# A ring of four load slots, other waits for the loads and a moved store wait in the ternary weight preparation of a Mamba-plus-BitLinear kernel

## The chip, the cores and the metric

One Trainium2 chip, eight cores. All cores run the same program on different data: core b gets sequence b of the input (2048 tokens of 1024 features) and its own copy of all weights. Nothing is exchanged between the cores. The time of a run is the device time of the slowest core in microseconds.

## The reference, cut to what matters

```python
def attn(x, Wd, bd, a_log, b_param, Wo, bo):          # per sequence
    delta = softplus(x @ Wd.T + bd)
    a_pos = softplus(a_log) + 1e-4                    # 1024 x 16 states
    # for each t: state = exp(-dt * a_pos) * state + dt * b_param * x_t
    #             y_t   = state.sum(-1)
    return y @ Wo.T + bo

def weight_quant(w):                                  # ternary weights
    scale = 1.0 / clip(mean(abs(w)), 1e-5)
    return clip(round(w * scale), -1, 1) / scale

def act_quant(x):                                     # 8 bit activations, scale by row
    scale = 127.0 / clip(max(abs(x), axis=-1), 1e-5)
    return clip(round(x * scale), -128, 127) / scale

def bitlinear(x, w):
    return act_quant(x) @ weight_quant(w).T

def ffn(x, w_gate, w_up, w_down):                     # 1024 -> 4096 -> 1024
    return bitlinear(silu(bitlinear(x, w_gate)) * bitlinear(x, w_up), w_down)

x = x + layernorm(attn(layernorm(x)))
x = x + layernorm(ffn(layernorm(x)))
```

The three weights of the second half (gate and up 4096 x 1024, down 1024 x 4096, float32, 16 MB each) are made ternary on the chip. That needs two passes over each weight: one for the mean of the absolute values, one to quantize.

## The kernel before, in words

**Order of work.** Each engine runs its own list of instructions in the order in which the program adds them (the class `Sched`, L29). An instruction waits on counters: `ST(engine)` is "the last counted instruction of that engine added so far", `sch.chain(engine)` the same on its own engine, and a DMA has a counter for its buffer slot. All loads and stores told of here are issued by SyncE (SP), whose list is in order too: a DMA that waits holds back every DMA behind it, and an engine that waits holds back all its later instructions.

**Stages.** (1) LayerNorm of x, the delta projection, and the scan of the first quarter of the tokens. (2) The weights of gate (`wg`) and then up (`wu`) are prepared by `prep_ternary_gen`. The program takes one step of this generator, then adds one block `emit_B_dc(1, dc)` of the scan of the second quarter (16 states: an exponential on ScalarE, a scan and a multiply-add on VectorE, and on GpSimd the save of the last state), then the next step. There are only 8 such blocks, so they stand between the first 9 steps of `wg`; all steps behind them stand alone. (3) `emit_C_q(0)`: output projection and LayerNorm of the first quarter, with the preparation of the down weight (`wdn`) between: after each of its four token tiles 6 steps are taken, and the steps left are taken at the end. (4) For each quarter of the tokens: gate and up projections, quantization, down projection, final LayerNorm; with the scans of the third and fourth quarter between.

**One weight in `prep_ternary_gen`.** Its memory is a buffer `wbuf` of 2 slots, each of 2 tiles of 128 x 1024 float32 (one load fills a slot: 1 MB), `tern` for ternary tiles, and `stage` for 256 transposed output columns.

- First pass (L472 to L491), 16 steps, q = 0 to 15: SyncE loads slot q % 2 (L478); ScalarE takes absolute values and their sum (L483); GpSimd adds the sum to `acc` (L488). For q of 2 and above the load waits for `ST("gpsimd")`, the last GpSimd instruction added: the add of step q-1, or where a scan block stands between, the last save added in it. The absolute values wait for the load, for `ST("gpsimd")` as well, and for ScalarE itself.
- Scale (L493 to L513): a chain of small instructions on TensorE, ScalarE and VectorE.
- Second pass (L533 to L590), per output row pair `rp`: the 2 slots' worth of tiles of `rp` are loaded again (L544), shifted and rounded by L552, made -1, 0 or 1 by L557 (both ScalarE), transposed by TensorE in pairs (L573), copied to `stage` by ScalarE (L529), and `stage` is stored to DRAM by SyncE (L586). Then ScalarE waits for that store to land (L589), as `stage` is written again by the next `rp`. Each load of this pass waits for `ST("scalar")`.
- `CC` is the number of 1024-wide tiles in a row of the weight. For gate and up `CC` is 1: 16 `rp` with one load of 2 tiles each, 8 copies to `stage`, and a store of 512 KB. For down `CC` is 4: 4 `rp` with 4 loads each (2 per half), 32 copies, and a store of 2 MB.

Of the kernel before, what the change touches and what calls it, by code (L numbers as in the profile page):

```python
# [7 lines left out]
F32 = mybir.dt.float32  # L8
# [117 lines left out]
def build_nc(stop_phase=99):  # L126
# [24 lines left out]
    with ExitStack() as es:  # L151
        S = lambda n, sh, dt: es.enter_context(nc.sbuf_tensor(n, sh, dt))
        sch = Sched(nc, es)
        ST = sch.token
# [46 lines left out]
        with nc.sbuf_tensor("aw1", [128, KC * NSTATE], F32) as aw1, \  # L201
# [3 lines left out]
                    waits=[t_nega_ld])  # L205
            sch.add("scalar", lambda h: h.activation(out=aw1[:], in_=aw1[:], func=AF.Exp, scale=-1.0),
                    waits=[sch.chain("scalar")])
            sch.add("scalar", lambda h: h.activation(out=aw1[:], in_=aw1[:], func=AF.Ln, bias=1.0),
                    waits=[sch.chain("scalar")])
            sch.add("scalar", lambda h: h.activation(out=aw2[:], in_=av, func=AF.Relu), inc=1)  # L210
            sch.add("vector", lambda h: h.tensor_tensor(aw1[:], aw1[:], aw2[:], ALU.add),
                    waits=[ST("scalar")])
            sch.add("vector", lambda h: h.tensor_scalar(av, aw1[:], 1e-4, -1.0, ALU.add, ALU.mult),
                    waits=[sch.chain("vector")])
# [136 lines left out]
        with nc.sbuf_tensor("lnscA", [128, D], F32) as lnscA, \  # L351
# [3 lines left out]
            with nc.psum_tensor("ptA", [128, KC, 1024], BF16) as ptA:  # L355
                for tc in range(NC):
# [5 lines left out]
                            waits=[t_st], inc=1)  # L362
                    t_ln = ST("scalar")
                    for ic in range(KC):
                        w = []
                        if ic == 0:
                            w.append(t_ln)
                            if tc >= 1:
# [4 lines left out]
                                waits=w, inc=(1 if ic == KC - 1 else 0))  # L373
# [5 lines left out]
                            waits=[t_pe], inc=1)  # L379
# [4 lines left out]
            with nc.psum_tensor("pdA0", [128, 512], F32) as pdA0, \  # L384
# [5 lines left out]
                for g in range(4):  # L390
                    for ec in range(KC):
# [5 lines left out]
                        par = it % 2  # L397
                        for kc in range(KC):
                            w = []
                            if kc == 0:  # L400
# [6 lines left out]
                                    waits=w, inc=(1 if kc == KC - 1 else 0))  # L407
# [4 lines left out]
                                waits=[t_mm])  # L412
                        sch.add("scalar", lambda h: h.activation(out=spA0[:], in_=spA0[:],
                                                                 func=AF.Exp, scale=-1.0),
                                waits=[sch.chain("scalar")])
                        sch.add("scalar", lambda h: h.activation(out=spA0[:], in_=spA0[:],
                                                                 func=AF.Ln, bias=1.0),
                                waits=[sch.chain("scalar")])
# [9 lines left out]
                                waits=[t_sp, sch.chain("vector")])  # L428
                        sch.add("scalar", None, waits=[ST("vector")])
                    t_mmw = ST("tensor")  # L430
                    for d in range(KC):
# [4 lines left out]
                            waits=([t_mmw] if d == 0 else []) + [sch.chain("vector")])  # L436
# [13 lines left out]
        def prep_ternary_gen(d_wsrc, d_wT, O, I, wsc_col, name, es_w):  # L450
            RC = O // 128
            CC = I // 1024
# [5 lines left out]
            else:  # L458
                wv4_slice = lambda q: _wv[:, q // 2, 2 * (q % 2):2 * (q % 2) + 2, :]
            wTv = d_wT.rearrange("(ic p) o -> p ic o", p=128)  # L460
            Sx = lambda n, sh, dt: es_w.enter_context(nc.sbuf_tensor(n, sh, dt))
            wbuf = Sx(f"{name}_buf", [128, 2, 2, 1024], F32)
            acc = Sx(f"{name}_acc", [128, 2], F32)
            tern = Sx(f"{name}_tern", [128, 2, I], BF16)
            stage = Sx(f"{name}_stage", [128, IC, 256], BF16)
# [1 line left out]
            sch.barrier()  # L467
            sch.add("gpsimd", lambda h: h.memset(acc[:, 0:1], 0.0),
                    waits=[sch.chain("gpsimd")])
            for q in range(RC * CC // 2):  # L470
                par = q % 2
                w_dma = []  # L472
                if q >= 2:
                    w_dma.append(ST("gpsimd"))
                else:
                    w_dma += [ST("gpsimd"), ST("scalar")]
                sch.dma("sync", f"wbuf{par}",
                        lambda h, q_=q, p=par: h.dma_start(  # L478
                            out=wbuf[:, p, :, :], in_=wv4_slice(q_)),
                        waits=w_dma)  # L480
                t_d = (f"dma_wbuf{par}", sch.counts[f"dma_wbuf{par}"])
                sch.add("scalar",
                        lambda h, p=par: h.activation(  # L483
                            out=tern[:].rearrange("p a b -> p (a b)")[:, 0:2048],
                            in_=wbuf[:, p, :, :].rearrange("p a b -> p (a b)"),
                            func=AF.Abs, accum_out=acc[:, 1:2]),
                        waits=[t_d, ST("gpsimd"), sch.chain("scalar")])
                sch.add("gpsimd", lambda h: h.tensor_tensor(acc[:, 0:1], acc[:, 0:1],  # L488
                                                            acc[:, 1:2], ALU.add),
                        waits=[ST("scalar"), sch.chain("gpsimd")])  # L490
                yield  # L491
            with nc.psum_tensor(f"{name}_p1", [1, 1], F32) as p1, \
# [4 lines left out]
                        waits=[ST("gpsimd")], inc=1)  # L497
                sch.add("scalar", lambda h: h.copy(out=sc2[:, 0:1], in_=p1[:]),  # L498
                        waits=[ST("tensor"), sch.chain("scalar")])
# [3 lines left out]
                        waits=[ST("scalar"), sch.chain("vector")])  # L503
                sch.add("vector", lambda h: h.reciprocal(sc2[:, 1:2], sc2[:, 0:1]),
                        waits=[sch.chain("vector")])
                sch.add("tensor", lambda h: h.matmul(p2[:], s_onesk[:], sc2[:],
                                                     start=True, stop=True),
                        waits=[ST("vector")], inc=1)
                sch.add("scalar", lambda h, wc=wsc_col: h.activation(
                    out=s_wsc[:, wc:wc + 2], in_=p2[:], func=AF.Copy),  # L510
                    waits=[ST("tensor"), sch.chain("scalar")])
# [5 lines left out]
            with nc.psum_tensor(f"{name}_pta", [128, 2, 1024], BF16) as pta, \  # L517
                 nc.psum_tensor(f"{name}_ptb", [128, 2, 1024], BF16) as ptb:
                pts4 = (pta, ptb)
                TPD = max(2 // CC, 1)  # L520
                bi = 0
                t_pe_hist = {}
                evac_args = {}
                evac_tok = {}

                def emit_evac(k):
                    half_, bb_ = evac_args[k]
                    sch.add("scalar",
                            (lambda p, b, pp: lambda h: h.activation(  # L529
                                out=stage_v[:, b * 2:(b + 1) * 2, p, :],  # L530
                                in_=pts4[pp][:, :, 0:128], func=AF.Copy))(half_, bb_, k % 2),
                            waits=[t_pe_hist[k], sch.chain("scalar")])
                    evac_tok[k] = ST("scalar")  # L533

                for rp in range(RC // 2):
                    for half in range(2):
                        r = rp * 2 + half
                        for c in range(CC):
                            gt = r * CC + c
                            if gt % 2 == 0:  # L540
                                q = gt // 2
                                par4 = q % 2
                                sch.dma("sync", f"wbuf{par4}",
                                        lambda h, q_=q, p=par4: h.dma_start(  # L544
                                            out=wbuf[:, p, :, :], in_=wv4_slice(q_)),
                                        waits=[ST("scalar")])
                            q = gt // 2
                            par4 = q % 2
                            tl = gt % 2
                            t_d = (f"dma_wbuf{par4}", sch.counts[f"dma_wbuf{par4}"])  # L550
                            sch.add("scalar",
                                    lambda h, p=par4, t_=tl: h.activation(  # L552
                                        out=wbuf[:, p, t_, :], in_=wbuf[:, p, t_, :],
                                        func=AF.Identity, scale=swcol, bias=s_magic_ap),
                                    waits=[t_d, t_magic, ST("tensor"), sch.chain("scalar")])
                            sch.add("scalar",
                                    lambda h, p=half, c_=c, pp=par4, t_=tl: h.activation(  # L557
                                        out=tern[:, p, c_ * 1024:(c_ + 1) * 1024],
                                        in_=wbuf[:, pp, t_, :], func=AF.Sign, bias=s_negm_ap),
                                    waits=[ST("tensor"), sch.chain("scalar")])  # L560
                            yield
                        ternv = tern[:].rearrange("p b (ic q) -> p b ic q", q=128)
                        t_q = ST("scalar")
                        for bb in range(IC // 2):
                            ppar = bi % 2
                            for j in range(2):
                                w = []
                                if j == 0:
                                    w.append(t_q)
                                    if bi >= 2:  # L570
                                        w.append(evac_tok[bi - 2])
                                sch.add("tensor",
                                        lambda h, p=half, i=bb * 2 + j, j_=j, pp=ppar: h.transpose(  # L573
                                            pts4[pp][:, j_, 0:128], ternv[:, p, i, :], s_ident[:]),
                                        waits=w, inc=1)
                            t_pe_hist[bi] = ST("tensor")
                            evac_args[bi] = (half, bb)
                            if bi >= 1 and (bi - 1) not in evac_tok:
                                emit_evac(bi - 1)
                            bi += 1  # L580
                            yield
                    if (bi - 1) not in evac_tok:
                        emit_evac(bi - 1)
                    t_ev = ST("scalar")
                    t_st2 = sch.dma("sync", "stage_st",
                                    lambda h, rp_=rp: h.dma_start(  # L586
                                        out=wTv[:, :, rp_ * 256:(rp_ + 1) * 256], in_=stage[:]),
                                    waits=[t_ev])
                    sch.add("scalar", None, waits=[t_st2])  # L589
                    yield  # L590
            sch.pe_fence()

        def make_prep_driver(queue):
# [171 lines left out]
        with nc.sbuf_tensor("s_h", [128, 4, DI], BF16) as s_h, \  # L765
# [14 lines left out]
            for g in range(4):  # L780
                with ExitStack() as es_gu:
# [5 lines left out]
                    for oc in range(8):  # L787
                        for half in range(2):
# [17 lines left out]
                            for c in range(4):  # L806
                                tc = g * 4 + c
                                for k4 in range(4):
                                    kc = half * 4 + k4
                                    w = []  # L810
# [314 lines left out]
```

How the kernel before makes its waits and increments, by code:

```python
        def emit_engine(handle, eng):  # L95
            for fn, waits, inc, inc_sem in self.ops[eng]:
                for (wname, wval) in waits:
                    if wval > 0:
                        handle.wait_ge(sems[wname], wval)
                if fn is not None:
                    instr = fn(handle)
                    if inc:
                        instr.then_inc(sems[inc_sem], inc)
```

## Time and profile before

| | |
|---|---|
| median of 3 runs | 4353.5 us (4347.38 to 4356.2) |
| the profiled execution | 4356.49 us |
| its slowest core, first to last instruction | 4354.9 us (core 6; others 4322.2 to 4348.9) |
| busy on that core | TensorE 1305.4 us, VectorE 1498.0 us, ScalarE 1449.5 us, GpSimd 260.0 us |
| DMA | 245.36 MB, mean 56 GB/s |
| preparation of `wg` and the scan blocks beside it | about 639 to 1294 us |
| preparation of `wu` | about 1294 to 1687 us |
| first quarter's output stage with the preparation of `wdn` | about 1687 to 2188 us |

The profile is of one execution. Busy times are sums over an engine; none is over 35% of the span, so the time is made of waits in chains of dependent work, and what matters is which wait ends last in each stage.

### The profile page before, as it was taken

The numbers are of one execution on the slowest core, as the hardware profiler recorded it, in microseconds if no ns is written. First come the engines' busy times: TensorE is split into PE (matmuls) and PEld (weight loads), VectorE is DVE, ScalarE is ACT, GpSimd is POOL, SyncE is SP. The second block draws the span as 40 slices with busy tenths as digits, with TensorE's granted clock in tenths as the row PEclk, the third lists the DMA queues.
The fourth block names the chain that finished last, engine by engine and source line by source line (L and its number), as shares of the span: only waits on it lengthen the run. The fifth ranks groups of instructions, "written<-read, shape, count | busy, mean of one in ns | idle before, by whom it ended". The sixth has DMA issues, their size and how long they took to land.

```text
span 4354.9 us, 25562 instructions; the slowest of 8 cores (4322.2 to 4354.9 us)
## 1 busy us (share of the span) xinstructions
PE 1305.4 (30%) x5260; PEld 530.6 (12%) x5260; DVE 1498.0 (34%) x2016; ACT 1449.5 (33%) x2106; POOL 260.0 (6%) x443
## 2 busy tenths in 40 slices
PE   1221210001110113001264460263541474626553
PEld 0100000000000001000021120121210132202221
DVE  0067748860000001000025796246794123021410
ACT  3544433333442443344522333322333311032101
POOL 0012212210000000000001121000000000000000
PEclk9965555555555555555587565686665695658766
DMA  4000010013233321323241011021011130112211
GB/s 62 0 0 1 0 29 29 20 53 105 93 97 135 97 87 48 106 86 97 77 136 49 15 53 39 7 91 48 30 39 39 39 107 20 48 39 78 68 39 48
DMA packets 164347, 245.36 MB, mean 56 GB/s; under 512 B 6113, under 2 KB 121058, under 8 KB 160098
## 3 DMA queue, kind: packets, MB, share of 16 engines
q1 hardware_dynamic: 159906, 235.07, 16.8%
q0 software_dynamic: 4288, 8.65, 1.3%
q8 instruction: 47, 0.77, 0.1%
q14 instruction: 106, 0.87, 0.1%
HBM read 218.80 MB, written 33.55 MB: 58 GB/s over the span
## 4 chain that ended last, share of the span: by engine, by line
DVE 26%; ACT 22%; PE 21%; DMA 17%; issue 9%; POOL 4%; DVEq 1%; ACTq 1%; SPq 0%; POOLq 0%
DVE s_sig L289 11%; PE pG L823 5%; PE pU L831 5%; PE pD L951 4%; DMA wg_buf<-wg 4%; DMA wu_buf<-wu 4%; DMA wdn_buf<-wdn 4%; POOL s_state L263 4%; DVE s_ytmp L313 4%; DVE s_sig L296 4%; DMA s_td<-tdT 2%; ACT s_h L913 2%; PE ptD L906 2%; PE pW L648 2%; DVE s_qs L855 2%
## 5 line engine op out<-in xcount | busy, mean ns | idle before, releaser
L282 ACT ACTIVATE s_abar<-s_dyq,s_nega 128x512 f32<-128x512 bf16 x512 | 369.4, 722 | 607.9 <-DVE s_sig L289 460.4
L289 DVE TENSOR_TENSOR_SCAN s_sig<-s_abar,s_state,s_lnf 128x512 bf16<-128x512 f32 x384 | 493.0, 1284 | 125.6 <-ACT s_abar L282 77.3
L951 PE MATMUL pD<-s_td,s_h 128*128 128x512 bf16 x1024 | 391.8, 567 | 217.0 <-DMA s_td<-tdT 213.4
L823 PE MATMUL pG<-s_tg,s_dyq 128*128 128x512 bf16 x1024 | 398.7, 389 | 136.7 <-DVE s_h L850 115.5
L831 PE MATMUL pU<-s_tu,s_dyq 128*128 128x512 bf16 x1024 | 398.0, 389 | 0.0
L313 DVE SCALAR_TENSOR_TENSOR s_ytmp<-s_sig,s_bprm,s_ytmp 128x512 bf16<-128x512 bf16 x448 | 336.5, 751 | 48.9 <-DVE s_sig L289 2.3
L850 DVE TENSOR_TENSOR s_h<-s_gtmp,pU 128x512 bf16<-128x512 bf16 x128 | 88.1, 688 | 712.0 <-ACT s_gtmp L843 712.0
L263 POOL TENSOR_TENSOR s_state<-s_sig,s_onesp 128x1 bf16<-128x1 bf16 x384 | 246.6, 642 | 1330.4 <-DVE s_sig L296 447.0
L843 ACT ACTIVATE s_gtmp<-pG,s_r1g 128x512 bf16<-128x512 f32 x128 | 87.9, 687 | 419.9 <-PE pU L831 250.2
L951 PEld LDWEIGHTS pD<-s_td,s_h 128*128 128x128 bf16 x1024 | 133.6, 135 | 474.2 <-issue 460.3
L648 PE MATMUL pW<-s_w,s_dyq 128*128 128x512 bf16 x256 | 91.8, 538 | 325.4 <-DVE s_x L668 198.6
L403 PE MATMUL pdA<-s_lnf,s_w 128*128 128x512 bf16 x256 | 91.7, 524 | 301.9 <-ACT spA L420 300.2
L906 PE MATMUL ptD<-s_ident,s_q2b 128*128 128x128 bf16 x512 | 74.9, 301 | 297.7 <-DVE s_q2b L897 186.0
L296 DVE TENSOR_TENSOR_SCAN s_sig<-s_abar,s_lnf 128x512 bf16<-128x512 f32 x128 | 156.8, 1225 | 20.1 <-ACT s_abar L282 7.2
L500 DVE TENSOR_SCALAR wu_sc<-wu_sc 1x1 f32<-1x1 f32 x1 | 0.1, 142 | 398.9 <-ACT wu_sc L498 398.9
L823 PEld LDWEIGHTS pG<-s_tg,s_dyq 128*128 128x128 bf16 x1024 | 102.0, 100 | 284.6 <-issue 181.0
L654 DVE TENSOR_TENSOR attnC<-pW,s_borep 128x512 f32<-128x512 f32 x16 | 11.1, 692 | 352.9 <-PE pW L648 352.6
L328 DVE TENSOR_SCALAR s_stats<-s_stats 128x1 f32<-128x1 f32 x48 | 7.4, 153 | 361.5 <-ACT lnscC L324 213.1
L913 ACT ACTIVATE s_h<-ptD 128x512 bf16<-128x512 bf16 x128 | 76.4, 597 | 145.8 <-PE ptD L906 145.8
L981 DVE TENSOR_SCALAR s_nt<-s_st 128x4 f32<-128x4 f32 x4 | 0.7, 170 | 347.0 <-ACT s_h L976 347.0
L963 ACT ACTIVATE s_dyq<-pD,s_r2d 128x1024 bf16<-128x1024 f32 x16 | 17.8, 1113 | 303.6 <-PE pD L951 302.3
L831 PEld LDWEIGHTS pU<-s_tu,s_dyq 128*128 128x128 bf16 x1024 | 102.0, 100 | 115.0 <-issue 10.4
(156 smaller groups left out, 1731.9 us busy)
## 6 DMA issues: line engine op xcount, KB each, us to landing
wg_buf<-wg SPq DMA_DIRECT2D x32, 1024.0 KB, 5.0
wu_buf<-wu SPq DMA_DIRECT2D x32, 1024.0 KB, 5.0
wdn_buf<-wdn SPq DMA_DIRECT2D x32, 1024.0 KB, 5.0
s_tg<-tgT SPq DMA_DIRECT2D x64, 512.0 KB, 3.7
s_tu<-tuT SPq DMA_DIRECT2D x64, 512.0 KB, 5.0
s_td<-tdT SPq DMA_DIRECT2D x64, 512.0 KB, 3.6
tgT<-wg_stage SPq DMA_DIRECT2D x16, 512.0 KB, 3.5
tuT<-wu_stage SPq DMA_DIRECT2D x16, 512.0 KB, 3.5
```

What stands on the lines that cost most here:

```text
L263: lambda h, c_=c_s, p=p_s: h.tensor_tensor(s_state[:, c_:c_ + 1], s_sig[:, p, QT - 1:QT], s_onesp[:], ALU.mult),
L282: lambda h, d=dc, n_=n, p=pa: h.activation(out=s_abar[:, p, :], in_=delta_view[:, d, t0:t0 + QT], func=AF.Exp, scale=s_nega[:, d, n_:n_ + 1]),
L289: lambda h, d=dc, c_=col, p=pa, s=ps: h.tensor_tensor_scan(s_sig[:, s, :], s_abar[:, p, :], lnT_view[:, d, t0:t0 + QT], s_state[:, c_:c_ + 1],
L296: lambda h, d=dc, p=pa, s=ps: h.tensor_tensor_scan(s_sig[:, s, :], s_abar[:, p, :], lnT_view[:, d, t0:t0 + QT], 0.0, ALU.mult, ALU.add),
L313: sch.add("vector", lambda h, d=dc, n_=n, s=ps: h.scalar_tensor_tensor(s_ytmp[:], s_sig[:, s, :], s_bprm[:, d, n_:n_ + 1], s_ytmp[:], ALU. ...
L403: lambda h, p=par, e=ec, k=kc, g_=g: h.matmul(psd[p][:], s_w[:, k, e * 128:(e + 1) * 128], lnT_view[:, k, g_ * 512:(g_ + 1) * 512], start= ...
L648: lambda h, k=kc, hf=half, t_=tc, p=pw: h.matmul(p[:], delta_view[:, k, t_ * 128:(t_ + 1) * 128], s_w[:, k, hf * 512:(hf + 1) * 512], star ...
L823: h.matmul(pGs[c_][:], q1T_view[:, k, t_ * 128:(t_ + 1) * 128], s_tg[:, wp, k4_, :], start=(k == 0), stop=(k == KC - 1)),
L831: h.matmul(pUs[c_][:], q1T_view[:, k, t_ * 128:(t_ + 1) * 128], s_tu[:, wp, k4_, :], start=(k == 0), stop=(k == KC - 1)),
L906: lambda h, j_=j: h.transpose(ptD[:, j_, 0:128], s_q2b[:, j_ * 128:(j_ + 1) * 128], s_ident[:]),
L913: lambda h, c_=c, o=osl: h.activation(out=q2T_view[:, c_, o * 4:(o + 1) * 4, :], in_=ptD[:, :, 0:128], func=AF.Copy),
L951: lambda h, c_=c, k=kc, p=par, s_=sub, f=hf: h.matmul(pDs[c_][:, f * 512:(f + 1) * 512], q2T_view[:, c_, k, :], s_td[:, p, s_, f * 512:(f ...
```

## The change

Three edits, all in `prep_ternary_gen`. `wbuf` gets 4 slots where `CC` is 1 (gate and up) and keeps 2 for down. Loads no longer wait for the latest instruction of GpSimd or ScalarE, but for the one that last read the slot: in the first pass the absolute values of step q - RING (`t_abs`), in the second pass the last L557 of load q - RING (`t_sign`), and for the first RING loads of the second pass still `ST("scalar")`. ScalarE's wait for the store of `stage` is moved from right behind the store to the first copy into `stage` of the next `rp` (`stage_guard`), and to the end for the last one.

```diff
--- before.py
+++ after.py
@@ -459,7 +459,8 @@
                 wv4_slice = lambda q: _wv[:, q // 2, 2 * (q % 2):2 * (q % 2) + 2, :]
             wTv = d_wT.rearrange("(ic p) o -> p ic o", p=128)
             Sx = lambda n, sh, dt: es_w.enter_context(nc.sbuf_tensor(n, sh, dt))
-            wbuf = Sx(f"{name}_buf", [128, 2, 2, 1024], F32)
+            RING = 4 if CC == 1 else 2
+            wbuf = Sx(f"{name}_buf", [128, RING, 2, 1024], F32)
             acc = Sx(f"{name}_acc", [128, 2], F32)
             tern = Sx(f"{name}_tern", [128, 2, I], BF16)
             stage = Sx(f"{name}_stage", [128, IC, 256], BF16)
@@ -467,13 +468,13 @@
             sch.barrier()
             sch.add("gpsimd", lambda h: h.memset(acc[:, 0:1], 0.0),
                     waits=[sch.chain("gpsimd")])
+            t_abs = {}
             for q in range(RC * CC // 2):
-                par = q % 2
-                w_dma = []
-                if q >= 2:
-                    w_dma.append(ST("gpsimd"))
+                par = q % RING
+                if q >= RING:
+                    w_dma = [t_abs[q - RING]]
                 else:
-                    w_dma += [ST("gpsimd"), ST("scalar")]
+                    w_dma = [ST("gpsimd"), ST("scalar")]
                 sch.dma("sync", f"wbuf{par}",
                         lambda h, q_=q, p=par: h.dma_start(
                             out=wbuf[:, p, :, :], in_=wv4_slice(q_)),
@@ -485,6 +486,7 @@
                             in_=wbuf[:, p, :, :].rearrange("p a b -> p (a b)"),
                             func=AF.Abs, accum_out=acc[:, 1:2]),
                         waits=[t_d, ST("gpsimd"), sch.chain("scalar")])
+                t_abs[q] = ST("scalar")
                 sch.add("gpsimd", lambda h: h.tensor_tensor(acc[:, 0:1], acc[:, 0:1],
                                                             acc[:, 1:2], ALU.add),
                         waits=[ST("scalar"), sch.chain("gpsimd")])
@@ -523,15 +525,22 @@
                 evac_args = {}
                 evac_tok = {}
 
+                stage_guard = [None]
+
                 def emit_evac(k):
                     half_, bb_ = evac_args[k]
+                    w = [t_pe_hist[k], sch.chain("scalar")]
+                    if stage_guard[0] is not None:
+                        w.append(stage_guard[0])
+                        stage_guard[0] = None
                     sch.add("scalar",
                             (lambda p, b, pp: lambda h: h.activation(
                                 out=stage_v[:, b * 2:(b + 1) * 2, p, :],
                                 in_=pts4[pp][:, :, 0:128], func=AF.Copy))(half_, bb_, k % 2),
-                            waits=[t_pe_hist[k], sch.chain("scalar")])
+                            waits=w)
                     evac_tok[k] = ST("scalar")
 
+                t_sign = {}
                 for rp in range(RC // 2):
                     for half in range(2):
                         r = rp * 2 + half
@@ -539,13 +548,14 @@
                             gt = r * CC + c
                             if gt % 2 == 0:
                                 q = gt // 2
-                                par4 = q % 2
+                                par4 = q % RING
                                 sch.dma("sync", f"wbuf{par4}",
                                         lambda h, q_=q, p=par4: h.dma_start(
                                             out=wbuf[:, p, :, :], in_=wv4_slice(q_)),
-                                        waits=[ST("scalar")])
+                                        waits=[t_sign[q - RING] if q >= RING
+                                               else ST("scalar")])
                             q = gt // 2
-                            par4 = q % 2
+                            par4 = q % RING
                             tl = gt % 2
                             t_d = (f"dma_wbuf{par4}", sch.counts[f"dma_wbuf{par4}"])
                             sch.add("scalar",
@@ -558,6 +568,8 @@
                                         out=tern[:, p, c_ * 1024:(c_ + 1) * 1024],
                                         in_=wbuf[:, pp, t_, :], func=AF.Sign, bias=s_negm_ap),
                                     waits=[ST("tensor"), sch.chain("scalar")])
+                            if tl == 1:
+                                t_sign[q] = ST("scalar")
                             yield
                         ternv = tern[:].rearrange("p b (ic q) -> p b ic q", q=128)
                         t_q = ST("scalar")
@@ -586,8 +598,10 @@
                                     lambda h, rp_=rp: h.dma_start(
                                         out=wTv[:, :, rp_ * 256:(rp_ + 1) * 256], in_=stage[:]),
                                     waits=[t_ev])
-                    sch.add("scalar", None, waits=[t_st2])
+                    stage_guard[0] = t_st2
                     yield
+            sch.add("scalar", None, waits=[stage_guard[0]])
+            stage_guard[0] = None
             sch.pe_fence()
 
         def make_prep_driver(queue):
```

## Rows read from the trace of the kernel before

**Rows 1.** The chain that ended last, on the page: shares of the span by engine.

```profile
DVE 26%; ACT 22%; PE 21%; DMA 17%; issue 9%; POOL 4%; DVEq 1%; ACTq 1%; SPq 0%; POOLq 0%
```

**Rows 2.** Engines by stretch: us from:to, length, busy us (instructions) by engine, clock, DMA.

```profile
639.00:954.20 315.20, 0.00 (x0) 0.00 (x0) 253.26 (x253) 108.36 (x144) 78.00 (x134) 0.50 0.08 27
...
1294.60:1414.00 119.40, 0.04 (x2) 0.07 (x2) 0.00 (x0) 32.03 (x32) 3.08 (x16) 0.50 0.41 141
...
2187.00:2340.00 153.00, 101.66 (x448) 43.78 (x448) 49.36 (x57) 32.57 (x44) 10.82 (x16) 0.86 0.33 103
```

**Rows 3.** Instructions in order of time where scan blocks meet: start, length, engine, line, [idle before].

```profile
677.24 0.70 POOL L263 TENSOR_TENSOR s_state<-s_sig,s_onesp 128x1 bf16<-128x1 bf16 x1 [1.54 <-DVE s_sig L289]
...
678.08 0.37 SPq L478 DMA_DIRECT2D wg_buf<-wg  x1
...
681.63 0.75 DVE L308 SCALAR_TENSOR_TENSOR s_dyq<-s_sig,s_bprm,s_ytmp 128x512 bf16<-128x512 bf16 x1
683.15 1.91 ACT L483 ACTIVATE wg_tern<-wg_buf 128x2048 bf16<-128x2048 f32 x1 [9.72 <-DMA wg_buf<-wg]
...
686.56 1.28 DVE L289 TENSOR_TENSOR_SCAN s_sig<-s_abar,s_state,s_lnf 128x512 bf16<-128x512 f32 x1 [4.17 <-POOL s_state L263]
```

**Rows 4.** The chain in order of time: load of step 8 of `wg` (start, us).

```profile
954.17 4.87 DMA wg_buf<-wg
```

**Rows 5.** First-pass ScalarE work by tile, `wg` then `wu`: ns min/median/max, first and last start.

```profile
L483 ACT ACTIVATE wg_tern<-wg_buf x16: 1909/1909/1910, 643.9 to 1012.1; 128x2048 bf16<-128x2048 f32 x16
...
L483 ACT ACTIVATE wu_tern<-wu_buf x16: 1909/1909/1910, 1299.4 to 1411.4; 128x2048 bf16<-128x2048 f32 x16
```

**Rows 6.** Timeline of the first pass of `wdn`.

```profile
1766.08 1.91 ACT L483 ACTIVATE wdn_tern<-wdn_buf 128x2048 bf16<-128x2048 f32 x1 [5.63 <-DMA wdn_buf<-wdn]
...
1768.29 0.19 POOL L488 TENSOR_TENSOR wdn_acc<-wdn_acc 128x1 f32<-128x1 f32 x1 [7.56 <-ACT wdn_tern L483]
...
1804.77 1.91 ACT L483 ACTIVATE wdn_tern<-wdn_buf 128x2048 bf16<-128x2048 f32 x1 [5.66 <-DMA wdn_buf<-wdn]
...
1820.20 1.91 ACT L483 ACTIVATE wdn_tern<-wdn_buf 128x2048 bf16<-128x2048 f32 x1
...
1859.22 1.91 ACT L483 ACTIVATE wdn_tern<-wdn_buf 128x2048 bf16<-128x2048 f32 x1 [5.83 <-DMA wdn_buf<-wdn]
```

**Rows 7.** The chain in order of time: second load of the first pass of `wdn`.

```profile
1768.61 4.96 DMA wdn_buf<-wdn
```

**Rows 8.** Timeline of the second pass of `wg`: store, next load, next ScalarE work.

```profile
1048.85 0.37 SPq L586 DMA_DIRECT2D tgT<-wg_stage  x1
1049.32 0.67 SPq L544 DMA_DIRECT2D wg_buf<-wg  x1
1056.05 1.24 ACT L552 ACTIVATE wg_buf<-wg_buf,s_const,s_wsc 128x1024 f32<-128x1024 f32 x1 [7.29 <-DMA wg_buf<-wg]
```

**Rows 9.** DMAs of the whole program: KB each, median us from issue to landing.

```profile
tgT<-wg_stage SPq DMA_DIRECT2D x16, 512.0 KB, 3.5
tdT<-wdn_stage SPq DMA_DIRECT2D x4, 2048.0 KB, 10.1
```

**Rows 10.** Who waited for `wdn_buf`: us in total, times.

```profile
  ACT wdn_buf L552: 110.5, 16
```

**Rows 11.** The chain in order of time: second-pass loads of one `rp` of `wdn`.

```profile
1975.54 12.61 DMA wdn_buf<-wdn
1993.52 5.06 DMA wdn_buf<-wdn
```

**Rows 12.** One microsecond within a load of `wg`: columns as in rows 2 (last: DMA share, GB/s).

```profile
965.00:966.00 1.00, 0.00 (x0) 0.00 (x0) 0.00 (x0) 0.00 (x0) 0.00 (x0) 0.50 1.00 414
```

**Rows 13.** Gate matmuls by tile: ns min/median/max.

```profile
L823 PE MATMUL pG<-s_tg,s_dyq x1024: 376/379/635, 2195.1 to 4083.1; 128*128 128x512 bf16 x171
```

**Rows 14.** Spans of the cores (the shortest and the longest).

```profile
core 5: 4322.2 us, clock 0.633
core 6: 4354.9 us, clock 0.628
```

## The prediction, made before the run

> **What bounds the kernel now.** I read the chain that ended last first. No engine holds more than about a quarter of it, and DMA holds 17% [rows 1]: far too much for 56 GB/s on average. In order of time nearly all of that DMA, up to 2188 us, is single loads of the weight buffers, each waited for alone. The stretches say the same: during the first pass of `wu` ScalarE is busy 32.03 of 119.40 us and the DMA engines 0.41 of the time, with nothing else at work [rows 2]. So load and use alternate where they could overlap. From 639 to 954 us the scan blocks are there too, and VectorE sets the pace: 253.26 of 315.20 us, a period of 39.4 us for each of 8 blocks.
>
> **First pass beside the scan blocks.** The load of a step waits for the save of state 13 of the block (ends 677.94 us) and goes out at 678.08; VectorE ends the block at 682.38, ScalarE starts the absolute values only at 683.15, and VectorE's next scan starts at 686.56, after 4.17 us idle [rows 3]. Afterwards the load landed long ago. ScalarE then waits only for that same save, and works from 678.1 to 680.2; the first exponential of the next block (108.36 us of ScalarE less 8 x 2.1, over 128: 0.72 us) [rows 2] is ready at 681, before VectorE ends its block at 682.4. The save of state 14 goes behind GpSimd's add and is ready by about 681.3. VectorE's gap falls to the 0.1 us that lies between any two of its instructions (61.9 us idle, less 7 x 4.17 and some 8 at the start, over 253) [rows 2]: 4.0 us saved at each of 7 joints, **28 us**. If something still keeps the 1.91 us of absolute values in the way, it is 2.0 us each, 14 us.
>
> **Rest of the first pass of `wg`.** The load of step 8 goes out at 954.17, and the last absolute values start at 1012.1: 57.9 us [rows 4, 5]. With everything loaded, a step lasts 1.91 us, the read of the sum, GpSimd's add, and two hand-overs: in `wdn` the add starts 2.21 us after the absolute values and takes 0.19 [rows 6], with the hand-over back 2.57 us. Steps 8 to 11 find their loads landed. Load 12 goes out 2.1 us after step 8 starts and each next one 2.6 later, against a need 10.3 us after step 8's start: in time. So 7 x 2.57 = 18 us in place of 57.9: **40 us**. If loads don't overlap and land 4.87 us apart [rows 4], the last starts after some 21.6: 36 us.
>
> **First pass of `wu`.** First to last absolute values: 1299.4 to 1411.4 us, 112.0 us for 15 steps, 7.47 each [rows 5]. Afterwards four loads are in flight, and the pace is the slower of 2.57 us (ScalarE and GpSimd) and the transfer of 1 MB. That transfer never shows undisturbed by its start: 0.41 x 119.40 / 16 gives 3.06 us of the engines' time per load [rows 2], and in its best microsecond a load moves 414 GB/s, which is 2.53 us [rows 12]. I take 3.0, nearer the share, since it includes slow starts: 15 x 3.0 = 45, **67 us** saved. Bounds: 2.57 each gives 73; 4.87 each, as if a load began only when the one before had landed, gives 39.
>
> The Trainium skill (HBM Reference, Specifications) says that the two cores of a pair share their memory's bandwidth and that each gets about 358 GB/s when both stream. That would make 2.93 us of a load where the row's best microsecond makes 2.53; by the page the saving is 68 us, by the row's rate ScalarE would bind at 2.57 and it is 73. No row here shows two cores streaming together.
>
> **First pass of `wdn`.** Two slots as before, but a load now waits for step q-2, so two are in flight. It runs in bursts of 6, 6 and 4 steps behind token tiles. Burst one: 1766.08 to 1804.77 us, 38.7 us for 5 steps; burst two: 1820.20 to 1859.22, 39.0 us, its first load being hidden behind the token tile [rows 6]. A load takes 4.96 us [rows 7], absolute values 2.1 until the next load may go. So every two steps take 4.96 + 2.1 = 7.1 us. Burst one: starts at 0, 2.9 (the second load follows by one transfer), 7.1, 10.1, 14.2, 17.4: 21 us saved. Burst two now finds two loads landed: 0, 2.57, 7.1, 10.0, 14.2, 17.2: 22. Burst three, 4 steps at the same spacing, 23 before and 10 now: 13. Together **56 us**; with landings 4.9 us apart 42.
>
> **Second pass of `wg` and `wu`.** Here I count nothing. Load `rp`+1 stands in SyncE's list behind the store of `rp`, and the store waits for the last copy to `stage`. Whatever the load's own wait says, it goes out right after the store: 1048.85 and 1049.32, needed at 1056.05, 7.29 us idle [rows 8]. Four slots don't change that order. The removed wait for the store is covered by the load: the store lands in 3.5 us at the median, 1052.4 [rows 9], the load is there 6.7 us after its issue. Where the wait now stands, at the first copy, the store has landed some 6 us ago. Without the cover of the load it would be worth those 3.5 us for each `rp`.
>
> **Second pass of `wdn`.** There ScalarE idles 110.5 us before L552 for 16 loads [rows 10]. In the later three `rp` the first load is queued behind a 2 MB store (10.1 us) and lands 12.61 us after its issue; the next take 5.06 and much the same [rows 9, 11]. About 5.4 us idle for each ordinary load and 13.5 for each behind a store gives 13 x 5.4 + 3 x 13.5 = 110.7, which fits. Afterwards loads 1 to 3 of an `rp` need only the slot's L557 two loads back. Load 1 goes out right behind load 0, lands one transfer (3.0) later, and is needed after two tiles of L552, 1.24 us each [rows 8], and of L557 over as much: some 4.8 us, an estimate. Hidden by 1.8. Loads 2 and 3 have a half of work in front of them: hidden. Load 0 stays behind the store. In the first `rp` load 1 still waits for `ST("scalar")`, so only two are hidden. That is 2 + 3 x 3 = 11 loads of 5.4: **59 us**. If load 1 in flight delays load 0 by a whole transfer, 3 x 3.0 less: 50.
>
> **Sum.** 28 + 40 + 67 + 56 + 59 = 250 us. The profiled execution took 4356.5, so 4106.5; the median of the runs shown lies 3.0 below it, so **4103.5, say 4104 us**. All bounds at their poor ends: 14 + 36 + 39 + 42 + 50 = 181, 4172 us. All at their good ends: 28 + 40 + 73 + 56 + 59 = 256, 4098. The work behind 2188 us is the same; but half of the span lies there and the cores differ by 33 us in all [rows 14], so I add 15 us either way for it. ScalarE, GpSimd and SyncE execute as many instructions as before; two more slot counters in the barriers cost nothing that a row shows.
>
> **Rivals.**
>
> *Loads hinder each other* (chance 0.18). Eight cores now load in bursts at up to three times the mean rate of before. For it: a load behind 0.5 MB of store lands in over 6 us instead of 5, one behind 2 MB in 12.61 [rows 8, 11]. Against: these are explained by bytes in front of it, and a microsecond at 414 GB/s exists [rows 12]. Time: landings 4.87 us apart, the poor ends: up to 4172; half way 4138.
>
> The Trainium skill (HBM Reference, Latency) gives 0.2 us for an access on average and 2 us at high load. With 1.8 us more for each load that is still waited for (1 in `wu`, 3, 2 and 1 in the bursts of `wdn`, 5 in its second pass) it would be 22 us more, 4126. No row here shows it.
>
> *The second passes of gate and up gain too* (0.02). If their loads did run ahead, 30 waits of some 7 us would go, less what the transfer leaves: about 200 us, 3905. SyncE's order speaks against it.
>
> *Nothing visible happens* (0.02): some wait I have not seen, such as the absolute values' wait for GpSimd, takes over each load's place. Against: between GpSimd's add and the absolute values there are always the 5 us of the load in the rows. 4353.
>
> *Slower: TensorE's clock* (0.03). The preparation runs at half clock, 1.2 GHz (0.50), and the gate and up stage behind it starts at 0.86 [rows 2]. Its matmuls take 376 ns at the one level and 635 at the worst [rows 13]; 2048 of them for gate and up. If the shorter preparation led to the low level there, each would cost up to 256 ns more, 524 us in all: 4628. It decides from 976 of the 2048 matmuls on (250 us / 0.256). Against: the engine idles in the same way ahead of that stage, only for less time.
>
> **How the numbers follow.** The sum as worked out has chance 0.75; its own range is 4080 to 4130. The range for 8 in 10 reaches from 4080 (good ends, less 15) to 4165 (into the first rival). This kernel's runs differ by 0.2% (9 us), so about that is what a measurement can tell from no change. Faster by over 0.2%: the sum, the first two rivals: 0.95. Within: 0.02. Slower: 0.03.
>
> **What the profile of the changed kernel would show.** The period of the scan blocks near 35.4 us, and no idle VectorE at the joints. First to last absolute values of `wu` near 45 us; 25 or below would break the step of 2.57, over 70 would mean loads in a row. Ahead of L552 of each `rp` in `wg` still some 7.3 us of idle time: if that falls, my reading of SyncE's list is wrong. In `wdn` one wait for each `rp` in the second pass, of some 13 us, and the later `rp` each 16 us shorter. The forecast fails most likely if landings of loads in flight together come later than 3.0 us apart, or if the half of the program behind 2188 us moves with TensorE's clock.

## The result, and the profile after

| | before | changed |
|---|---|---|
| median | 4353.6 us (8 runs, 4347.38 to 4359.92) | 4148.01 us (8 runs, 4143.01 to 4153.4) |
| ratio | | 0.953 (95%: 0.9519 to 0.954) |
| slowest core of the profiled run | 4354.9 us (core 6) | 4143.9 us (core 3) |

The change saves 205.6 us where I forecast 249.5 (4353.5 to 4104). The time is 44 us above the forecast. It lies inside the range for 8 in 10 (4080 to 4165), but outside the sum's own range (4080 to 4130). On the page, the chain that ended last holds 14% DMA in place of 17% [rows 1], and every other engine's share is within one point of what it was.

Where the saving comes from shows best in one table of stretches, cut at the same instructions in both kernels. Core 6 is read in both. It was the slowest core before, and is not quite the slowest after, so its own saving is larger: 213.6 us (4354.9 less 4141.3). Of these 209.8 are in the table, and the other 3.8 stand ahead of it, where no edit reaches. These are the stretches of core 6 after (us from:to, length, then TensorE, its weight loads, VectorE, ScalarE and GpSimd busy, granted clock, DMA share, GB/s):

```profile
635.20:959.20 324.00, 0.74 (x4) 0.61 (x4) 257.59 (x258) 124.72 (x162) 85.38 (x142) 0.50 0.15 52
959.20:1235.40 276.20, 45.22 (x256) 17.58 (x256) 0.00 (x0) 125.57 (x192) 0.10 (x1) 0.50 0.29 91
1235.40:1305.50 70.10, 0.74 (x4) 0.61 (x4) 0.29 (x2) 32.35 (x34) 3.09 (x16) 0.50 0.69 239
...
1650.60:1747.60 97.00, 3.08 (x20) 2.00 (x20) 6.74 (x22) 45.26 (x54) 3.47 (x18) 0.50 0.50 173
1747.60:1963.40 215.80, 48.13 (x264) 18.22 (x264) 3.68 (x12) 132.01 (x202) 0.00 (x0) 0.50 0.33 107
1963.40:4141.30 2177.90, 1009.85 (x3872) 412.57 (x3872) 916.21 (x1298) 570.03 (x827) 85.14 (x128) 0.68 0.16 51
```

| stretch | before | after | saved | forecast |
|---|---|---|---|---|
| gate, first pass with the scan blocks, and scale | 377.8 | 324.0 | 53.8 | 28 + 40 = 68 |
| gate, second pass | 277.8 | 276.2 | 1.6 | 0 |
| up, first pass and scale | 121.5 | 70.1 | 51.4 | 67 |
| up, second pass, and output projection | 344.8 | 345.1 | -0.3 | 0 |
| down, first pass and scale, with token tiles | 141.5 | 97.0 | 44.5 | 56 |
| down, second pass | 275.6 | 215.8 | 59.8 | 59 |
| everything behind the last store of the preparation | 2176.9 | 2177.9 | -1.0 | 0 |

Busy times of TensorE, VectorE and ScalarE in each stretch are the same in both kernels to within 1%, save for the clock's part behind 1963 us: only waits went. The shortfall lies in the three first passes: 14.2 + 15.6 + 11.5 = 41.3 us.

The main cause can be read from ScalarE's first steps of `wu` (start, length, engine, line, what, [idle before, released by]):

```profile
1240.32 1.91 ACT L484 ACTIVATE wu_tern<-wu_buf 128x2048 bf16<-128x2048 f32 x1 [9.05 <-DMA wu_buf<-wu]
...
1248.88 1.91 ACT L484 ACTIVATE wu_tern<-wu_buf 128x2048 bf16<-128x2048 f32 x1 [6.57 <-DMA wu_buf<-wu]
...
1256.37 1.91 ACT L484 ACTIVATE wu_tern<-wu_buf 128x2048 bf16<-128x2048 f32 x1 [5.48 <-DMA wu_buf<-wu]
...
1264.00 1.91 ACT L484 ACTIVATE wu_tern<-wu_buf 128x2048 bf16<-128x2048 f32 x1 [5.63 <-DMA wu_buf<-wu]
...
1266.55 1.91 ACT L484 ACTIVATE wu_tern<-wu_buf 128x2048 bf16<-128x2048 f32 x1 [0.54 <-POOL wu_acc L490]
...
1300.77 1.91 ACT L484 ACTIVATE wu_tern<-wu_buf 128x2048 bf16<-128x2048 f32 x1 [1.23 <-DMA wu_buf<-wu]
```

Steps 0 to 3 are as far apart as before or a little more, 7.5 to 8.6 us against 7.47; only from step 3 on is the pace new: 12 steps in 36.8 us, 3.06 each. Below, this is called the serial start: the first RING loads of a pass go out one at a time, and each is waited for alone. What held SyncE in the first pass of `wg` stands in its list of waits (waiter, released by: us in total, times, longest):

```profile
SPq L99 <- ACT wg_tern L484: 187.4, 9, 35.4
SPq L99 <- POOL s_state L263: 116.7, 3, 39.1
```

Three loads, 1 to 3, still waited for the saves of a scan block, as [rows 3] shows for the kernel before; from load 4 on SyncE waits for ScalarE's absolute values four steps back. Where the new wait is at work, the joint between two scan blocks looks as forecast. VectorE is at a gap of 0.1 us (L308 ends at 832.74, the next scan starts at 832.84), and the load goes out with nobody waiting for it:

```profile
828.44 1.91 ACT L484 ACTIVATE wg_tern<-wg_buf 128x2048 bf16<-128x2048 f32 x1 [4.67 <-POOL s_state L263]
...
830.51 0.37 SPq L479 DMA_DIRECT2D wg_buf<-wg  x1
...
831.98 0.76 DVE L308 SCALAR_TENSOR_TENSOR s_dyq<-s_sig,s_bprm,s_ytmp 128x512 bf16<-128x512 bf16 x1
...
832.84 1.28 DVE L289 TENSOR_TENSOR_SCAN s_sig<-s_abar,s_state,s_lnf 128x512 bf16<-128x512 f32 x1
```

In the second pass of gate almost nothing moved; ScalarE waits for each of 16 loads as before (7.29 us for the one in [rows 8]; 113.6 us in total before). After:

```profile
ACT wg_buf L562 <- DMA wg_buf<-wg: 111.3, 16, 7.6
```

### The profile page after: what moved, and what is told of

It reads as the page before. It is cut to its first block, busy times and chain, and to the rows that moved or that the text cites. A ratio compares the mean times of both kernels' runs of the same rounds, so it can differ in the third digit from the quotient of the medians.

```text
span 4143.9 us, 25572 instructions; the slowest of 8 cores (4120.7 to 4143.9 us)
## 1 busy us (share of the span) xinstructions
PE 1296.4 (31%) x5260; PEld 530.1 (13%) x5260; DVE 1497.5 (36%) x2016; ACT 1451.1 (35%) x2106; POOL 265.7 (6%) x443
## 4 chain that ended last, share of the span: by engine, by line
DVE 26%; ACT 22%; PE 22%; DMA 14%; issue 10%; POOL 5%; ACTq 1%; DVEq 1%; SPq 0%; POOLq 0%
DVE s_sig L289 11%; PE pG L837 5%; PE pU L845 5%; POOL s_state L263 5%; PE pD L965 5%; DVE s_sig L296 4%; DMA wu_buf<-wu 4%; DMA wg_buf<-wg 3%; DVE s_ytmp L313 3%; DMA s_td<-tdT 2%; DMA wdn_buf<-wdn 2%; ACT s_h L927 2%; PE ptD L920 2%; PE pW L662 2%; DVE s_qs L869 2%
## 5 line engine op out<-in xcount | busy, mean ns | idle before, releaser
L965 PE MATMUL pD<-s_td,s_h 128*128 128x512 bf16 x1024 | 376.0, 549 | 210.8 <-DMA s_td<-tdT 207.2
L845 PEld LDWEIGHTS pU<-s_tu,s_dyq 128*128 128x128 bf16 x1024 | 102.5, 100 | 117.5 <-issue 14.2
```

The source lines that it names most:

```text
L845: h.matmul(pUs[c_][:], q1T_view[:, k, t_ * 128:(t_ + 1) * 128], s_tu[:, wp, k4_, :], start=(k == 0), stop=(k == KC - 1)),
L965: lambda h, c_=c, k=kc, p=par, s_=sub, f=hf: h.matmul(pDs[c_][:, f * 512:(f + 1) * 512], q2T_view[:, c_, k, :], s_td[:, p, s_, f * 512:(f ...
```

## The experiments

All are compared with the kernel before, run beside them on the same chip; its median there was 4351.71 us in the first group (1 to 4) and 4352.08 in the second (5 to 8). The changed kernel was not run again in either group, so a distance from its 4148.01 us carries some 2 us more of uncertainty: that is how far these two medians lie from the 4353.6 above. The diffs are cut to the lines that matter.

**1. First loads set free.** In the changed kernel the first RING loads of the first pass keep the old wait for `ST("gpsimd")`, that is for the step before them.

```diff
-                    w_dma = [ST("gpsimd"), ST("scalar")]
+                    w_dma = [ST("gpsimd"), ST("scalar")] if q == 0 else []
```

> The changed kernel, but loads 1 to RING-1 of the first pass have no wait of their own (in the changed kernel they still wait for the last GpSimd and ScalarE instruction added, so that loads 0 to 3 of gate and up and 0 and 1 of down run one at a time). Theory 'serial start': the 44 us that my forecast was too low are these loads. Then the three joints between scan blocks that still stall (4.1 us each) close: 12 us; in up three steps of 7.5 us become steps of about 3.2: 13 us; in down one step of 8.5 us becomes 3: 5 us. Together some 30 us below the changed kernel's 4148: 4118. Rival 'loads hinder each other': the steps only get slower behind it, and less than 8 us is gained: 4140 to 4150.

Measured: 4120.36 us, ratio 0.9466 (0.9453 to 0.9479), 27.7 us below the changed kernel. So the serial start cost that much, and the rival's 8 us or less is excluded. On core 6 the stretches of the table shrink by 9.7 us (gate), 12.1 (up) and 5.9 (down), where 12, 13 and 5 were expected. The first pass of `wu` takes 47.0 us from its first to its last absolute values (1234.6 to 1281.6), where 45 were forecast; it was 60.5 in the changed kernel and 112.0 before [rows 5]. During these 47 us the DMA engines are all but full, so transfers set the pace now, 3.13 us for each load:

```profile
1234.60:1281.60 47.00, 0.00 (x0) 0.00 (x0) 0.00 (x0) 30.03 (x30) 2.89 (x15) 0.50 0.96 329
```

**2. Two slots everywhere.**

```diff
-            RING = 4 if CC == 1 else 2
+            RING = 2
```

> The changed kernel with 2 slots for gate and up too; all other edits stay. Theory 'serial start': a smaller ring has only one serial load in place of three (8 us won at the joints of the scan blocks, 8 us at the start of up), and loses in the steps behind, since two loads in flight give a step of (5 to 6 + 2.1)/2, about 3.8 us, in place of 3.2: about 8 us lost in up and 5 us in gate. So about the same as the changed kernel, 4138 to 4155. Rival 'the four slots carry the gain': without them gate and up lose most of what they won in the first pass, 4200 or more.

Measured: 4150.76 us, ratio 0.9537 (0.9524 to 0.955), 2.8 us above the changed kernel and 201 below the one before it. With the serial start in place, two more slots gain less than measurements tell apart (the two ratios' intervals overlap). Absolute values of `wu` take 66.7 us there (1243.5 to 1310.2), 6.2 more than with four slots; gate's stretch takes 325.7 us in place of 324.0. More slots shorten the steps (from the end of the serial start on, 4.20 us each in `wu` with two slots, 3.06 with four), and each slot adds a load to the serial start. What two slots do with the first loads set free was not run.

**3. Only the moved store wait.** The kernel before, with `stage_guard` as in the change and nothing else.

> The kernel before with only the moved store wait. Prediction's step: the load behind the store covers it, nothing is gained: 4353 within 0.2%. Rival 'the store wait costs': up to 3.5 us for each of 32 row pairs of gate and up and more in down, some 100 us or more: 4250.

Measured: 4354.45 us, ratio 1.0008 (0.9999 to 1.0017). The edit is worth nothing by itself. ScalarE's idle time ahead of the shifting and rounding of `wg` stays with the load (busy us, mean ns | idle before, released by):

```profile
L558 ACT ACTIVATE wg_buf<-wg_buf,s_const,s_wsc 128x1024 f32<-128x1024 f32 x32 | 39.7, 1240 | 112.0 <-DMA wg_buf<-wg 110.4
```

**4. Only the new waits of second-pass loads.**

```diff
-                                        waits=[ST("scalar")])
+                                        waits=[t_sign[q - 2] if q >= 2
+                                               else ST("scalar")])
...
+                            if tl == 1:
+                                t_sign[q] = ST("scalar")
```

> The kernel before with only the new waits of the second-pass loads (t_sign), two slots everywhere. Prediction's step: gate and up gain nothing, since each load stands behind the store in SyncE's list; down loses 11 waits of 5.4 us: 59 us, 4294. Rival 'second passes of gate and up gain too': 150 us or more on top, below 4150.

Measured: 4296.52 us, ratio 0.987 (0.9855 to 0.9885): 55 us, against 59 forecast. The second pass of `wdn` takes 218.7 us in place of 275.6, that of `wg` 277.9 as before:

```profile
1899.90:2118.60 218.70, 48.04 (x264) 18.23 (x264) 3.69 (x12) 132.03 (x202) 0.00 (x0) 0.50 0.34 106
1015.70:1293.60 277.90, 45.17 (x256) 17.57 (x256) 0.00 (x0) 125.55 (x192) 0.10 (x1) 0.50 0.29 91
```

**5. Second-pass loads ahead of the store in SyncE's list.** The waits stay those of the change; only the place in the list changes. RING loads are issued at the start of the second pass, and each later one right behind the L567 that frees its slot.

```diff
+                def emit_load2(q, waits):
+                    if q < RC * CC // 2:
+                        t_load2[q] = sch.dma("sync", f"wbuf{q % RING}", ..., waits=waits)
+                for q in range(RING):
+                    emit_load2(q, [ST("scalar")])
...
                             if tl == 1:
                                 t_sign[q] = ST("scalar")
+                                emit_load2(q + RING, [t_sign[q]])
```

> The changed kernel, but in the second pass a load is put into SyncE's list right behind the L567 that frees its slot (RING loads at the start), so ahead of the store of that row pair. Theory: gate and up gained nothing there only because each load stands behind a store. Then the 7.3 us idle of each of 30 row pairs shrinks to what the store still costs (landing 3.5 us or a little more, less the 3 us until the first copy to stage: 0.5 to 2.5 us), and in down 3 waits of 13 us and one of 5 go: 190 to 230 us below the changed kernel, 3920 to 3960. Rival 'transfers are the limit' (loads and stores hinder each other): the row pairs stay above 14 us, less than 100 us gained, 4050 or more.

Measured: 3916.24 us, ratio 0.8995 (0.898 to 0.901): 232 us below the changed kernel, 4 us past the good end of what was expected. The rival (less than 100 us) is excluded. The 16 waits of `wg` for a load are down to one, the first, and the store has become visible in their place:

```profile
ACT wg_stage L537 <- DMA tgT<-wg_stage: 20.6, 12, 2.9
...
ACT wg_buf L566 <- DMA wg_buf<-wg: 5.2, 1, 5.2
```

**6. All loads ahead.** Experiments 1 and 5 together, and the first RING loads of the second pass wait only for the absolute values that last read their slot.

```diff
+            NQ = RC * CC // 2
+            for q in range(RING):
+                emit_load2(q, [t_abs[NQ - RING + q]])
             with nc.psum_tensor(f"{name}_p1", [1, 1], F32) as p1, \
```

> e5_order, with the first-pass loads free from the start as in e1_free_first, and the first RING loads of the second pass waiting only for the absolute values that last read their slot, so that they land during the scale chain. Expected 28 us less for the first, as measured in e1_free_first, and 3 x 5.2 us = 15 us for the loads behind the scale chains: some 43 us below e5_order, near 3895.

Measured: 3872.73 us, ratio 0.8894 (0.8877 to 0.8912), 43.5 us below experiment 5, where some 43 were expected. (The expected 3895 was counted from the middle of the range expected for experiment 5, before its time was known.)

**7. The store wait put back.** Experiment 6 with ScalarE's wait right behind the store, as in the kernel before.

```diff
-                    stage_guard[0] = t_st2
+                    sch.add("scalar", None, waits=[t_st2])
                     yield
-            sch.add("scalar", None, waits=[stage_guard[0]])
```

> e6_all_ahead with ScalarE's wait for the store put back right behind the store. In the kernel before that wait was covered by the load behind the store. Theory: with that cover gone, it costs the time in which ScalarE could have quantized: some 2.5 to 3 us for each of 32 row pairs of gate and up, up to 10 us for each of 3 or 4 of down: 110 to 130 us above e6_all_ahead. Rival 'the store wait costs nothing anyway': within 10 us of it.

Measured: 3993.9 us, ratio 0.9177 (0.9161 to 0.9192): 121.2 us above experiment 6. The same edit that gained nothing in experiment 3 is worth 121 us once no load covers it. The wait in `wg` (waiter, released by: us in total, times, longest):

```profile
ACT wg_buf L567 <- DMA tgT<-wg_stage: 61.5, 15, 5.6
```

**8. Two `stage` buffers for gate and up.** Experiment 6, and the store of one `rp` has a whole `rp` to land.

```diff
+            NST = 2 if CC == 1 else 1
-            stage = Sx(f"{name}_stage", [128, IC, 256], BF16)
+            stage = Sx(f"{name}_stage", [128, NST, IC, 256], BF16)
```

> e6_all_ahead with two stage buffers for gate and up, so that the store of one row pair has a whole row pair of time to land. If the store still ends last at the first copy in e6_all_ahead (0.5 to 2.5 us for each row pair), 15 to 75 us are gained; if ScalarE is the limit there already, nothing within 5 us.

Measured: 3850.07 us, ratio 0.8844 (0.8831 to 0.8858), 22.7 us below experiment 6 and the fastest version here: 298 us below the changed kernel. In the second pass of `wg` ScalarE is busy 125.4 us of the 162.4 from its first shift to the last store, where the same stretch took 268.6 us before (1021.8 to 1290.4):

```profile
950.70:1113.10 162.40, 45.17 (x256) 17.53 (x256) 0.00 (x0) 125.39 (x192) 0.00 (x0) 0.50 0.44 139
```

## Why the prediction was right, and where it was off

- **What bounds the kernel.** Right. Only waits for single loads went, and what stands behind the last store of the preparation (at 2178.0 us before) takes 2177.9 us in place of 2176.9, at the same clock of 0.68.
- **The first pass: the step that was mis-sized.** "Afterwards four loads are in flight", "the second load follows by one transfer" and "Afterwards the load landed long ago" for 7 joints are true only from load RING on. I took the new wait for all loads; the diff leaves the old one on the first RING. In gate 3 of 7 joints still stall (3 x 4.0 = 12 us), in up 3 steps stay at 7.5 to 8.6 us (8.56 + 7.49 + 7.63 = 23.7 us for what was forecast as 9), in down one step of 8.5 us stands for one of 2.9. These give 12 + 15 + 6 = 33 us of the 44. The sum has no term for this, and no rival either. Setting the loads free gave back 27.7 (experiment 1), not all 33: they then queue for the same DMA engines, and the first of up is used 6.3 us after its issue in place of 4.9.
- **What is left of the 44.** Experiment 1 is 16 us above the forecast. Its gate, up and down first passes, scale included, take 314.3, 58.0 and 91.1 us, so they save 63.5, 63.5 and 50.4 where 68, 67 and 56 were forecast, and the second pass of down saves 56 in place of 59: 4.5 + 3.5 + 5.6 + 3 = 16.6 us. In up the step measured 3.13 us against 3.0. In down the term "every two steps take 4.96 + 2.1 = 7.1 us" was too small: it gives a load that shares the DMA engines with another the time of a lone one. In burst one of the changed kernel the loads that ScalarE waited for behind the serial start landed 6.7 and 6.1 us after their issue, and two steps took 9.2 and 8.4 us (absolute values of steps 1, 3 and 5 at 1664.27, 1673.51 and 1681.88 us). I had given this a chance as "loads hinder each other". It is there, but mild: not 4.87 us a load.
- **Luck in the range.** The room from 4130 up to 4165 was left for loads that hinder each other, and they cost some 9 us (3.5 in up, 5.6 in down). What carried the time into that room was the serial start, which I had not seen. That the range holds the time is in part luck.
- **Rest of gate's first pass.** Right where the loads were ready: steps 8 to 15 took 18.85 us from first to last in the changed kernel (935.67 to 954.52), forecast 18. The first of the seven steps took 3.57 us, the other six 2.55 each, and in those ScalarE waited for GpSimd's add alone (0.54 us a step).
- **Second passes of gate and up.** Right for the reason given. Freeing the wait of a load moves nothing while it stands behind a store in SyncE's list (experiment 4); moving it in the list gives the gain (experiment 5).
- **Store wait.** Right that it is covered (experiment 3), and near on its worth without cover: I wrote 3.5 us for each `rp`. In experiment 7 ScalarE stood idle for 61.5 / 15 = 4.1 us at each store of `wg`. The edit doesn't win all of that, for in experiment 6 ScalarE still waits 21.0 us in total for stores, at the first copies. From its first shift to its last store the second pass of `wg` takes 221.4 us with the wait put back and 172.9 without: 48.5 us, 3.0 for each of 16 `rp`.
- **Second pass of down.** Right: 59.8 us in the trace; 55 by the times of experiment 4 alone, 56.9 in its trace.
- **Transfer rate.** I took 3.0 us for 1 MB. Experiment 1 shows 329 GB/s at a share of 0.96, and 3.13 us a load. Its trace also shows what slows the loads. Core 6, with all eight cores loading, and later with only half of them:

```profile
1238.00:1268.00 30.00, 0.00 (x0) 0.00 (x0) 0.00 (x0) 19.03 (x19) 1.73 (x9) 0.50 0.99 333
...
1276.00:1278.00 2.00, 0.00 (x0) 0.00 (x0) 0.00 (x0) 1.49 (x1) 0.00 (x0) 0.50 1.02 418
```

From 1238 to 1268 us every core moves 329 to 333 GB/s at a share of 0.99 to 1.01. From 1276 to 1278 cores 2, 4 and 7 move nothing any more and core 1 only 80 GB/s, and cores 0, 3, 5 and 6 move 395 to 424 at a share of 1.01 to 1.03 (the profile's share can come out a little over 1; each core's time is counted from its own first instruction). The 16 DMA engines of a core are busy throughout in both, so it is not their own speed that holds the loads at 333, but something that the cores share. The Trainium skill (HBM Reference, Specifications) says about 358 GB/s for each core when both of a pair stream; an estimate from that page's figure is 2.93 us for 1 MB. With all cores streaming, the trace lies 7 to 8% below the page. That the shared thing is the memory of a pair is not shown: no trace here tells which cores are a pair.

- **The other rivals.** The clock did not fall (gate and up matmuls on core 6 average 389 to 390 ns after, 389 before). The wait for GpSimd took no load's place: in the first passes it held ScalarE for 4.8 us in gate, 1.6 in up and 2.2 in down.

## What to carry to other kernels

Here a load went out when its own wait was met and every DMA before it in SyncE's list had been issued (freeing the wait alone left the second pass of `wg` at 277.9 us against 277.8, experiment 4; moving the loads ahead of the stores won 232 us over the whole kernel, experiment 5). So loosen a load's wait only together with its place in the list, above all where a store that ends a chain stands in front of it. When a ring is deepened, look at how the first turns through it are treated: if they keep the old wait, each added slot adds a serial load, and four slots here were worth no more than two (4148.0 us and 4150.8). A wait that costs nothing may be covered by another; price it again once the cover is gone (0 us in one kernel, 121 us in the next).

## What the runs showed of the hardware

With up to four loads of 1 MB queued (first pass of `wu`, experiment 1), a load lands 10.0 us after its issue at the median (6.2 to 14.7), where one alone takes 5.0 (kernel before), yet one lands every 3.13 us. Three loads ahead of it at 3.13 us each are 9.4 us, so the landing time of a queued load is mostly its turn in the queue. A longer landing time is no sign of a slower pass: the median landing of `wu` loads rose from 5.0 to 6.3 us in the changed kernel, while the pass got shorter. A load issue behind the 2 MB store of 512-byte rows held SyncE for up to 5.4 us where 0.33 is usual, before and after:

```profile
L553 SPq DMA_DIRECT2D wdn_buf<-wdn x16: 327/328/5374, 1747.6 to 1935.2; - x16
```

In experiment 5, where the loads stand ahead of that store, the longest such issue is 0.72 us. Why the issue takes so long was not tested.
